# Sixteen weight tiles in four groups of four, a two-pass fp32r delta and no negated copy

## The reference

```python
lora_delta = lora_B @ lora_A * 0.5               # rank 64, 2048 x 2048
cb = codebook / max(|codebook|)                  # 32 levels
scale = exp(scale_log)                           # one per output row and 128 inputs
normalized = (weight + lora_delta).reshape(O, 16, 128) / scale
idx = searchsorted((cb[:-1] + cb[1:]) / 2, normalized)
w_eff = cb[idx] * scale + lora_delta             # rounding of the straight-through form aside
y = x @ w_eff.T
base, ax, logits = y @ W_base.T + b_base, y @ A_w.T, y @ router_w.T
mixed = sum over experts e of softmax(logits)[e] * (ax @ cores[e])
out = x + base + mixed @ B_w.T * 2
```

## Time and profile before

| | us |
|---|---|
| median of three runs | 2498.5 |
| the profiled execution | 2502.43 |
| its span, first to last instruction | 2500.6 |
| PE busy | 2373.2 |
| DVE busy | 1795.6 |
| ACT busy | 1499.5 |
| POOL busy | 1203.9 |

### The profile page before, as it was taken

How to read it: one execution, slowest core, us unless ns; L and a number is a source line. 1 busy time by engine, 2 the same in 40 slices (tenths; PEclk the granted TensorE clock), 3 DMA queues, 4 the chain that set the end, 5 groups by cost and what they waited for, 6 DMA issues and landing times.

```text
span 2500.6 us, 31530 instructions
## 1 busy us (share of the span) xinstructions
PE 2373.2 (95%) x11808; PEld 2129.7 (85%) x11808; DVE 1795.6 (72%) x2274; ACT 1499.5 (60%) x1906; POOL 1203.9 (48%) x742
## 2 busy tenths in 40 slices
...
GB/s 157 184 231 182 206 201 214 183 141 143 250 288 294 286 257 115 114 135 211 238 227 231 226 169 103 119 143 218 223 238 212 211 142 131 140 215 234 237 239 199
DMA packets 141981, 493.06 MB, mean 197 GB/s; under 512 B 15058, under 2 KB 75986, under 8 KB 100818
## 3 DMA queue, kind: packets, MB, share of 16 engines
...
HBM read 305.91 MB, written 185.07 MB: 196 GB/s over the span
## 4 chain that ended last, share of the span: by engine, by line
PE 77%; DVE 11%; ACT 5%; issue 2%; POOL 2%; DMA 2%; SPq 0%; DVEq 0%; POOLq 0%; ACTq 0%
PE m L621 17%; PE m L622 17%; PE m L623 17%; DVE acc L879 9%; PE m L605 8%; PE m L606 8%; PE m L607 8%; PE pd L559 2%; ACT mk L739 2%; PE m L651 1%; DMA part<-part 1%; ACT mp L749 1%; POOL pp L1024 1%; ACT ds L727 1%; DVE kl L906 1%
## 5 line engine op out<-in xcount | busy, mean ns | idle before, releaser
L879 DVE SCALAR_TENSOR_TENSOR acc<-mk,dj,acc 128x1024 f32<-128x1024 uint8 x800 | 1025.1, 1281 | 117.8 <-ACT mk L739 53.6
L739 ACT ACTIVATE mk<-wr,bj 128x1024 uint8<-128x1024 f32 x800 | 902.6, 1143 | 232.7 <-DVE acc L879 222.5
L621 PE MATMUL m<-gh,xh 128*128 128x384 f32 (+2 forms) x2560 | 913.7, 357 | 25.6 <-DVE part L896 11.3
L622 PE MATMUL m<-gl,xh 128*128 128x384 f32 (+2 forms) x2560 | 902.6, 353 | 0.0
L623 PE MATMUL m<-gh,xl 128*128 128x384 f32 (+2 forms) x2560 | 900.3, 352 | 0.0
L621 PEld LDWEIGHTS m<-gh,xh 128*128 128x128 f32 x2560 | 484.2, 189 | 84.2 <-issue 24.7
L623 PEld LDWEIGHTS m<-gh,xl 128*128 128x128 f32 x2560 | 483.7, 189 | 23.4
L622 PEld LDWEIGHTS m<-gl,xh 128*128 128x128 f32 x2560 | 484.8, 189 | 20.6
L1020 POOL TENSOR_SCALAR tm<-mp,dj 128x1024 f32<-128x1024 uint8 x192 | 218.3, 1137 | 452.6 <-ACT mp L749 448.3
L901 DVE TENSOR_TENSOR part<-m,part 128x384 f32<-128x384 f32 (+2 forms) x480 | 280.2, 585 | 215.3 <-PE m L623 214.8
L605 PE MATMUL m<-kh,wh 128*128 128x384 f32 (+2 forms) x1120 | 398.6, 356 | 25.6 <-DVE kl L906 17.4
...
## 6 DMA issues: line engine op xcount, KB each, us to landing
...
```

The lines of the kernel that those rows point to most:

```text
L621: e.matmul(R.m[c][:, 0:w], xh, gh, start=k == 0, stop=False)
L622: e.matmul(R.m[c][:, 0:w], xh, gl, start=False, stop=False)
L739: e.activation(R.mk[k % NM], w, ACT.Identity, bias=R.bj[:, j:j + 1], scale=GROW).then_inc(S["mk"], 1)
L879: e.scalar_tensor_tensor(R.acc, R.mk[k % NM], R.dj[:, j:j + 1], R.acc, ALU.mult, ALU.add).then_inc(S["ac"], 1)
```

## The change

- `GROUP` is 4, 4, 4, 4. Startup now holds halves 0 to 8 and makes four tiles of G in fp32. The token stages of groups 0, 1 and 2 hold 7, 6 and 6 halves, the weight stages 2, 2 and 0.
- The negated copy is gone. Step 0 of a half computes mask times step minus the half itself, from two operands in SBUF.
- Seven steps of a half are POOL's (`NP`), 24 DVE's, and POOL's places in the list are (0, 3, 6, 10, 13, 16, 19).
- Delta: lora_B stands twice on 128 rows and is split in a high and a low fp32r part, lora_A stands high on rows 0 to 63 and low on rows 64 to 127, and each piece is two fp32r matmuls. The first eight pieces of the program use two PSUM banks and come before the first step. Eight further pieces fall in half 0, four in half 1, eight in halves 6 to 8, forty in halves 9 to 13. The buffers lie where the high parts of the weights will, so splitting starts after half 13.
- Partial sums are loaded one block ahead at a chunk 0, not two ahead at a chunk 3.

```diff
-NP = 6
+NP = 7
-SPARE_AT = (0, 3, 9, 13, 17, 21)
+SPARE_AT = (0, 3, 6, 10, 13, 16, 19)
+NORM_AT, SPLIT_EVERY = 8, 6
-GROUP = (2, 3, 4, 4, 3)
+GROUP = (4, 4, 4, 4)
-LOOK0, LOOK = 1, 2
+LOOK0 = 1
+UNTIL_TOKENS, UNTIL_WEIGHTS = (16, 24, 32), (0, 18, 26, 32)
+class Background:
+    def level(self, consumed):
+        yield ("unit", self.q, self.j)
+        if self.j % SPLIT_EVERY == SPLIT_EVERY - 1 and (self.q, self.j) > LAST_DELTA:
+            yield from self.splits(min(self.q, self.split + 1), consumed)
+        self.j += 1
+        if self.j == NV:
+            yield ("effect", self.q)
+            self.q, self.j = self.q + 1, 0
+    def levels(self, until, share, consumed):
+        left = NV * (until - self.q) - self.j
+        for _ in range(max(0, left - int(self.total * (1 - share)))):
+            yield from self.level(consumed)
...
 def delta_places():
+    late = [(0, j) for j in range(2, NV, 3)] + [(1, j) for j in range(4)]
+    late += [(q, j) for q in range(2 * N0 - 2, 2 * N0 + 1) for j in range(3)][:8]
+    late += [(q, j) for q in range(2 * N0 + 1, NQ) for j in range(1, NV, 3)]
+    return dict(zip(late, range(EARLY, NDELTA)))
...
 # sync
+    e.dma_start(R.cb, io["cb"].partition_broadcast(128)).then_inc(S["cb"], 16)
     e.dma_start(R.sc, io["sl"]).then_inc(S["sl"], 16)
...
+                if g and 2 <= t < NT - 1:
+                    load_part(g, t + 1)
                 if t:
                     store_part(g, t - 1)
-            if c == 3 and g and t and t + 2 < NT:
-                load_part(g, t + 2)
...
 # tensor
+    def wide(n):
...
+        e.matmul(bank[:, 0:w], R.lbh[:, ot], R.las[:, first:first + w], start=True, stop=False)
+        e.matmul(bank[:, 0:w], R.lbl[:, ot], R.las[:, first:first + w], start=False, stop=True).then_inc(S["pd"], 1)
...
 # scalar
-        if j == 1:
-            if q:
-                e.wait_ge(S["cl"], q)
-            e.activation(R.acc, w, ACT.Copy, scale=-1.0).then_inc(S["neg"], 1)
...
 # vector
         if j == 0:
-            e.wait_ge(S["neg"], q + 1)
+            if q:
+                e.wait_ge(S["cl"], q)
+            e.scalar_tensor_tensor(R.acc, R.mk[k % NM], R.dj[:, j:j + 1], R.wr[raw_of(q)], ALU.mult,
+                                   ALU.subtract).then_inc(S["ac"], 1)
```

More of the change, by code:

```diff
@@ L71, in group_of @@
     return next(g for g in range(NG) if FIRST[g] <= b < FIRST[g + 1])
-def units(q):
-    for j in range(NV):
-        yield ("unit", q, j)
-        if j == 8 and q not in (2 * b for b in FIRST):
-            yield ("split", q - 1)
-    yield ("effect", q)
 def startup():
@@ L94, in startup, with __init__, splits, begin @@
     yield ("rows_out", N0 - 1)
-def weights_of(g, ahead):
-    late = [ev for ev in ahead if ev[0] == "split"]
-    ahead = [ev for ev in ahead if ev[0] != "split"]
-    done = 0
+class Background:
+    def __init__(self):
+        self.q, self.j, self.split = 2 * N0 + LOOK0, 0, 2 * N0
+    def level(self, consumed):
[6 more added lines that the diff above has]
+            self.q, self.j = self.q + 1, 0
+    def splits(self, until, consumed):
+        while self.split < until and self.split - HIGH < consumed:
+            yield ("split", self.split)
+            self.split += 1
+    def levels(self, until, share, consumed):
+        left = NV * (until - self.q) - self.j
+        for _ in range(max(0, left - int(self.total * (1 - share)))):
+            yield from self.level(consumed)
+    def begin(self, until):
+        self.total = NV * (until - self.q) - self.j
+def weights_of(g, back):
+    until = UNTIL_WEIGHTS[g]
+    back.begin(until)
     for s in range(NS):
@@ L107, in weights_of, with tokens_of @@
             yield ("x_first", g)
-        goal = max(done, min(len(ahead), len(ahead) * (s + 1) // (NS - 6)))
-        yield from ahead[done:goal]
-        done = goal
-    yield from late
-def tokens_of(g, rest):
-    done = 0
+        yield from back.levels(until, min(1.0, (s + 1) / (NS - 6)), 2 * FIRST[g])
+def tokens_of(g, back):
+    until = UNTIL_TOKENS[g]
+    back.begin(until)
     for t in range(NT):
@@ L119, in tokens_of @@
             yield ("chunk", g, t, c)
-            goal = max(done, min(len(rest), len(rest) * (NCH * t + c + 1) // (NT * NCH - 10)))
-            yield from rest[done:goal]
-            done = goal
-    yield ("split", 2 * FIRST[g + 2] - 1)
+            yield from back.levels(until, min(1.0, (NCH * t + c + 1) / (NT * NCH - 10)), 2 * FIRST[g + 1])
+    yield from back.splits(2 * FIRST[g + 2], 2 * FIRST[g + 1])
     yield ("close", g)
@@ L147, in walk @@
     yield from startup()
-    ready = 2 * N0 + LOOK0
+    back = Background()
     for g in range(NG):
         if g:
-            ready = 2 * FIRST[g + 1] + (LOOK if g < LAST else 0)
-            yield from weights_of(g, [ev for q in range(2 * FIRST[g + 1], ready) for ev in units(q)])
+            yield from weights_of(g, back)
         if g < LAST:
-            yield from tokens_of(g, [ev for q in range(ready, 2 * FIRST[g + 2]) for ev in units(q)])
+            yield from tokens_of(g, back)
     yield from last_tokens()
@@ L406, in delta_in @@
         pairs = 8 * ((b - 1) // 4) + 4 * h + 4
-        for p in range(2):
-            e.wait_ge(S[f"ds{p}"], 16 * (pairs // 2))
+        for p in range(NDS):
+            e.wait_ge(S[f"ds{p}"], 16 * len(range(p, pairs, NDS)))
         e.wait_ge(S["we"], q - 1)
@@ L685, in mix @@
         e.matmul(R.pm[0:96, 0:128], R.cr, R.zt, start=True, stop=True).then_inc(S["pm"], 1)
-    direct(0, 0)
-    direct(0, 1)
+    narrow(0, 0)
+    narrow(0, 1)
+    for n in range(EARLY):
+        wide(n)
+    narrow(1, 0)
+    narrow(1, 1)
     for ev in walk():
@@ L752, in split @@
         e.wait_ge(S["we"], q + 1)
+        if q == 2 * N0:
+            e.wait_ge(S["pd"], UNITS)
+            e.wait_ge(S["lal"], len(QUAD))
+            for p in range(NDS):
+                e.wait_ge(S[f"ds{p}"], 16 * len(range(p, NDELTA // 2, NDS)))
         if q - HIGH >= 2 * N0:
```

191 lines of the change are left out of this document (112 added, 79 removed), and 2 rows, old and new, of the table COMPUTE.

## The result

The changed kernel takes 2444.65 us (median of four runs, 2440.47 to 2445.1) against 2498.53: ratio 0.978, interval 0.9763 to 0.9797. The forecast was 2438. The profiled execution took 2445.1 us with a span of 2443.3, where the prediction put 2442 and 2440.5.

A forecast was written before the change was run, and what follows sets the result against it. PE was taken to bound full token stages, but not startup, where POOL, DVE and ACT do. Terms +126.0, +134.4, +97.2 and -417.7 sum to -60.1, taking 2498.5 to 2438 us; range 2414 to 2478.

The forecast's parts named there:

- PE's pace: Token stages: PE itself sets 2.83 us for a tile and a block, 362.2 us for four tiles.
- Halves 1 to 8: Startup: POOL's circle plus contention give 37.1 us a half, 299 us for the eight (bounds 289 and 315).
- POOL's circle: Startup halves: POOL's scaling, delta, seven steps and normalising take 36.1 us, longer than DVE's 34.8.
- the collision: Startup: step 0's two SBUF operands contend with POOL's L1029; DVE waits 1.9 us or POOL 1.28.
- Lead-in: Before DVE's first step: it begins at 22 us instead of 24.21 (bounds 20 and 27).
- Half 0: First half of startup: 37 us instead of 56.7 (bounds 35 and 44), ACT's masks and piece copies taking 36.2.
- Token stage of group 0: First token stage: 381 us, from 362.2 for four tiles, 16.6 for forty delta pieces on PE and 2 more.
- the crowd about half 14: First token stage: four weight splits put POOL near 50 of its 48 us, covered by 8 us of list levels.
- Weight stages: Between token stages: 187 us in group 1 (before 158.2), 186 for the last, without quantising.
- The negated copy: Startup: without it DVE needs 34.8 us a half (37.2 before) and could start 3.1 us earlier; contention counts against it.
- Rival 4: Startup: PE's fp32 rows at half clock make a half 60 us, 2621 us in all; chance 0.05.

The follow-up runs named there:

- the dense kernel: The changed kernel with the twelve delta pieces of halves 0 and 1 at levels 2 to 13 of half 0, one a level instead of one in three: 2450.94 us.

## Why the prediction was right

- **PE's pace.** 2.83 us for a tile and a block held to 0.1 us in token stages 1 and 2, and the last stage came to 406.8 for 407.9. Reading the stages one by one, and not PE's 95% of the span, is what made the sum.
- **Halves 1 to 8.** The step was right in kind, POOL's circle with its seventh step, and the contention. It was 4.7 us short, and not because of the collision where POOL is the bound: halves 2 and 4 took 36.9 for 37.1. In the three halves with a row tile split off DVE is the bound and has to carry the 2.3 and the 1.7, 38.7 each, 4.8 us over 37.1 in the three, for which I had allowed 2 with the pieces of halves 6 to 8 in it. Half 1 took 38.5, and 36.9 in the dense kernel, where it has no pieces; I had put its four pieces at nothing. Half 8 took 37.9. My two terms for the collision, 1.9 on DVE or 1.28 on POOL, were meant as one or the other; it costs both, DVE 1.68 and POOL 0.86.
- **Lead-in.** 24.0 for 22: I took DVE's work on the scales for undisturbed, and POOL's splits lengthen it (L392 and L394, 4.7 us in place of 0.35).
- **Half 0.** 37.8 for 37, with ACT busy throughout, as in my sum of its work (36.2). Where PE is slow or a buffer late it grows at once, as the dense kernel shows.
- **Token stage of group 0.** 384.0 for 381. The pieces cost 16.6 us on PE, as worked out; 3.6 of the other 5.2 us come from the crowd about half 14, which I had called covered: I had looked at POOL's steps there and not at the low part of x behind them. The clock behind PE's two stops has about 3 of the 5.2 us (about 1.5 of those 3.6, and the 1.5 of the first block); the prediction had no term for it.
- **Weight stages.** Six us better than forecast in stages 1 and 2. I had priced the copy's removal in startup alone; in the weight stages DVE's step 0 waited for it, with the low part of the weights behind.
- **The negated copy.** The prediction's terms made its removal worth 2.5 us a half less what contention takes. In the kernel before that balance is a loss, in the changed one it costs 2.0 us in startup and 2.5 in token stage 0, and wins 4 in each of two weight stages. By the spans that is 3.8 us won, and most of it by a path that the prediction did not name.
- **Rival 4.** The granted clock in startup was 0.86 and 0.87, PE's rows took about 30 us of each half, and no half came near 44.6.

The errors nearly cancel: +7.5 in startup, +3 in token stage 0, -5 in the weight stages, -1 at the end, and what is left in the gaps; the span is 2.8 us longer than forecast. Of the other 3.9 us of the 6.7, 3.4 are the step from the profile to the median (before's profiled execution stood 3.9 us above its median, and this one stands 0.5 above, so the difference of the spans, 57.3, is not that of the medians, 53.9), and the rest is rounding. That the total is within 0.3% is in part luck.
